# Reading score tables back tile by tile behind the scatters, and attention of the last tile in pieces, in a two-layer graph network on one Trainium2 core

## The reference, cut to what matters

```python
# edges come sorted by dst; dst is drawn as 625 * u**2, so low nodes have the most edges
xl = (x @ W_l).reshape(625, 4, 64)
xr = (x @ W_r).reshape(625, 4, 64)
e = xl[src] + xr[dst]
e = where(e >= 0, e, 0.2 * e)
score = einsum('ehd,hd->eh', e, att)              # 20000 edges x 4 heads
m = segment_max(score, dst)
ex = exp(score - m[dst])
alpha = ex / (segment_sum(ex, dst)[dst] + 1e-16)
agg = segment_sum(alpha[:, :, None] * xl[src], dst)
h = elu(agg + bias) + x
gnn = layernorm(h) * gamma + beta
...
x = x + gnn + mix(xn)
logits = layernorm(x) @ gate_w + gate_b           # top 2 of 16 experts
...
```

## Time and profile before

| | |
|---|---|
| median of three runs | 1079.36 us (1077.4 to 1082.58) |
| profiled execution, its own time | 1083.8 us |
| span of its trace | 1082.0 us |
| mean granted TensorE clock | 0.877 |
| busy: PE, DVE, ACT, POOL | 851.8, 774.3, 353.6, 380.2 us |
| 16 DMA engines, mean over the span | 120 GB/s |

### The profile page before, as it was taken

One profiled execution on the slowest core, in us unless ns is written; L12 is line 12 of the kernel. 1 busy time (PEld: TensorE's weight loads), 2 busy tenths in 40 slices (PEclk: granted clock), 3 DMA queues, 4 the chain that ended last, 5 costly groups with the idle time before them and its releaser, 6 DMA issues.

```text
span 1082.0 us, 18242 instructions
## 1 busy us (share of the span) xinstructions
PE 851.8 (79%) x5483; PEld 744.8 (69%) x5483; DVE 774.3 (72%) x1980; ACT 353.6 (33%) x1004; POOL 380.2 (35%) x321
## 2 busy tenths in 40 slices
PE   4888778977999880078459999769893895799996
PEld 2578666766778770078359999755793685788985
DVE  7778878788775880079888887576979656766635
ACT  0377444444663452056011111001560171121120
POOL 3288476776777677200022222410000000311204
PEclk9988889887999995577669999888897897799999
DMA  8830000000000000593059999750000001788883
GB/s 290 260 129 2 2 3 3 3 4 2 4 3 3 3 3 2 137 237 91 24 182 331 322 331 330 253 193 1 1 2 0 1 2 32 293 291 300 303 312 98
DMA packets 38278, 129.35 MB, mean 120 GB/s; under 512 B 12885, under 2 KB 20929, under 8 KB 29913
## 3 DMA queue, kind: packets, MB, share of 16 engines
q1 hardware_dynamic: 21742, 112.64, 31.3%
q0 software_dynamic: 10464, 8.67, 4.8%
q10 hardware_dynamic: 5992, 7.04, 1.9%
HBM read 108.83 MB, written 19.26 MB: 118 GB/s over the span
## 4 chain that ended last, share of the span: by engine, by line
PE 54%; DVE 23%; DMA 10%; issue 6%; POOL 4%; ACT 2%; SPq 0%; DVEq 0%; POOLq 0%; ACTq 0%
PE bank L862 12%; PE bank L651 7%; PE bank L873 6%; PE bank L583 4%; PE bank L795 3%; DMA arena<-pair_scores 3%; POOL arena L2281 2%; DVE tc L1281 2%; PE bank L629 2%; DMA pair_scores<-arena,pair_cells 2%; PE bank L961 2%; PE bank L784 2%; DVE cnt L1275 2%; PE bank L669 2%; DVE arena L1287 2%
## 5 line engine op out<-in xcount | busy, mean ns | idle before, releaser
L2247 POOL DMA_INDIRECT pair_scores<-arena,pair_cells x184 | 230.0, 1250 | 107.5 <-issue 57.3
L2271 POOL DMA_INDIRECT arena<-row_tab,ids x42 | 57.6, 1371 | 498.6 <-DVE ids L1664 491.7
L862 PE MATMUL bank<-arena 128*128 128x128 f32 x1480 | 182.5, 282 | 2.8 <-DMA arena<-in_exp 2.8
L862 PEld LDWEIGHTS bank<-arena 128*128 128x128 f32 x1480 | 177.1, 199 | 4.2 <-DMA arena<-in_exp 3.1
L651 PE MATMUL bank<-x_hi,hot 125*125 x368 | 119.6, 350 | 6.5 <-issue 0.7
L2011 ACT ACTIVATE tc<-bank 125x256 f32<-125x256 f32 x184 | 70.7, 385 | 136.4 <-PE bank L651 126.1
L651 PE MATMUL bank<-x_lo,hot 125*125 x368 | 106.1, 307 | 0.0
L873 PE MATMUL bank<-arena 128*128 128x256 f32 (+1 forms) x404 | 97.4, 384 | 0.0
L784 PE MATMUL bank<-ident,arena 125*125 125x125 f32 x260 | 46.0, 310 | 65.1 <-ACT arena L2058 63.7
L651 PEld LDWEIGHTS bank<-x_hi,hot 125*125 125x125 f32 x368 | 76.9, 209 | 20.1 <-issue 17.7
L784 PEld LDWEIGHTS bank<-ident,arena 125*125 125x125 f32 x260 | 41.2, 219 | 69.6 <-issue 57.7
(11 more groups left out here) (395 smaller groups left out, 1693.0 us busy)
## 6 DMA issues: line engine op xcount, KB each, us to landing
arena<-in_exp SPq DMA_DIRECT2D x25, 1024.0 KB, 6.8
arena<-in_exp SPq DMA_DIRECT2D x17, 1386.0 KB, 6.3
arena<-in_exp0o SPq DMA_DIRECT2D x25, 512.0 KB, 6.9
pair_scores<-cnt SPq DMA_DIRECT2D x10, 1093.8 KB
arena<-in_exp1o SPq DMA_DIRECT2D x17, 640.0 KB
arena<-pair_scores SPq DMA_DIRECT2D x7, 1093.8 KB
slot_y<-arena ACTq DMA_DIRECT2D x34, 128.0 KB, 6.3
fmaps<-pair_scores SPq DMA_DIRECT2D x3, 1093.8 KB
```

Of the source, the lines that this page charges most:

```text
L862: mm = pe.matmul(banks[1 + 2 * q + buf][0:rows, i * SLOTS:(i + 1) * SLOTS], w_in(s, q, k, m, rows), xsT[:, s, k, :], start=(k == 0), stop= ...
L2247: p.indirect_dma_start(out=pair_scores[which], in_=sc_ring[:, i, which, :], in_offset=None, out_offset=bass.IndirectOffsetOnAxis(ap=pair_c ...
L2271: p.indirect_dma_start(out=xs[:, q, :], out_offset=None, in_=tab, in_offset=bass.IndirectOffsetOnAxis(ap=ids[:, q, :], axis=0))\
```

## The change

SP no longer waits for all scatters. It reads from `ends_i` how many scatters of each table have to land until the blocks of a tile are complete; with these edges 38, 53, 66 and 76 of 92 for tiles 0 to 3, and 78, 80, 82 and 84 for the first four src pieces of tile 4. `ends_i` is a new row of eight integers, made in the sort by one more matmul on PE and five small operations on DVE. Tile m is loaded when its count is reached and its buffers are free (`h2` counts up to 3 at the three steps of the mix block named above, whose memory the new buffers share). The load of a tile is cut into pieces of 32, 32, 32 and 29 rows for each table (`PACED`), and each DMA is issued when the one before has landed, one at a time. The last tile comes in five pieces by src tile, of 112 and 13 rows x 2,000 B for each table, the fifth after all scatters; its maxima are taken over four pieces first and over the fifth behind them (`last_maxima`). The ring `masked` gets a fourth slot in this layer. The order on DVE, and the cut of the transposes ahead of the gate (`LATE`: tiles 0 to 3, then tile 4, in place of `CHUNKS`: tiles 0 to 2, then 3 and 4), follow from that.

```diff
+BASES["ends"] = BASES["order"] + BUCKETS
+ENDS = [T * m for m in range(1, T)] + [T * (T - 1) + s for s in range(1, T)]
+PACED = tuple(slice(r, min(r + 32, P)) for r in range(0, P, 32))
+LATE = [(0, (T - 1) * P, tuple(range(T - 1))), ((T - 1) * P, P, (T - 1,))]
...
-        SDENSE = [(0, 1), (5, 6), (2, 3), (4, 1), (0, 6)]
+        SDENSE = [("a0", "tde"), ("f1", "f0"), ("a1", "a2"), ("a3", "tab"), ("f0", "a2")]
...
+                at = BASES["ends"]
+                pe.matmul(banks[4][0:1, 2 * SORTED:2 * SORTED + len(ENDS)], begins, orders[:, at:at + len(ENDS)],
+                          start=True, stop=True).then_inc(sem("sorted"), 1)
...
+                rounded_of(ends_f[:, :], banks[4][0:1, 2 * SORTED:2 * SORTED + len(ENDS)], 0.5, -0.25)
+                own.link(v.tensor_scalar(ends_f[:, :], ends_f[:, :], 16.0, 16.0, ALU.mult, ALU.add))
+                v.tensor_scalar(ends_i[:, :], ends_f[:, :], float(16 * PAIRS), None, ALU.min).then_inc(sem("sorting"), 1)
...
+                    if i == MIX["m2"]:
+                        dve.sem_inc(sem("h2"), 1)
...
+            def merge_piece(s):
+
+                dve.wait_ge(sem(f"sdense{T - 1}"), (s + 1 if s == T - 1 else T - 1) * 2 * 16 * len(PARTS))
+                first, second = (sdense[q][:, s * P:(s + 1) * P, :] for q in SDENSE[T - 1])
+                own.note(v.tensor_tensor(first, first, second, ALU.max))
+
+            def last_maxima(part):
...
+                for h in range(H):
+                    i = m * H + h
+                    a, b, low = (0, cut, rneg) if part == 0 else (cut, N, rneg_a)
+                    after(dve, sem("l0_prob"), i - 3)
+                    own.note(v.tensor_tensor_reduce(masked_l0[:, i % 4, a:b], first[:, a:b, h], cnt[:, m, a:b], -1.0, -LOWEST,
+                                                    ALU.add, ALU.min, low[:, i:i + 1]))
+                    if part == 1:
+                        own.fence()
+                        v.tensor_tensor(rneg[:, i:i + 1], rneg[:, i:i + 1], rneg_a[:, i:i + 1], ALU.min)\
+                            .then_inc(sem("l0_max"), 1)
...
             average(2)
             add_elu(1)
-            table_maxima(4)
+            for s in range(T - 1):
+                merge_piece(s)
             average(3)
             add_elu(2)
-            add_normed(0, 1, 2)
-            average(4)
+            last_maxima(0)
             add_elu(3)
-            add_elu(4)
-            add_normed(3, 4)
-            norm_again(*range(T))
+            merge_piece(T - 1)
+            last_maxima(1)
+            add_normed(0, 1, 2, 3)
+            average(T - 1)
+            norm_again(0, 1, 2, 3)
+            add_elu(T - 1)
+            add_normed(T - 1)
+            norm_again(T - 1)
+            late_from_fm(0)
...
+            def await_scatters(end):
+
+                landed = sp.value_load(ends_i[0:1, end:end + 1], min_val=8, max_val=16 * PAIRS)
+                for w in range(2):
+                    sp.wait_ge(sem(f"scattered{w}"), landed)
+
+            def load_table(m):
+
+                n = 0
+                for w in range(2):
+                    for rows in PACED:
+                        sp.dma_start(sdense[SDENSE[m][w]][rows, :, :].rearrange("p n h -> p (n h)"), cells[w][m][rows])\
+                            .then_inc(sem(f"sdense{m}"), 16)
+                        n += 16
+                        sp.wait_ge(sem(f"sdense{m}"), n)
...
+            sp.wait_ge(sem("sorting"), SORTING["ends"])
+            sp.wait_ge(sem("h2"), 1)
+            await_scatters(0)
+            load_table(0)
+            sp.wait_ge(sem("h2"), 2)
+            await_scatters(1)
+            load_table(1)
+            sp.wait_ge(sem("h2"), 3)
+            await_scatters(2)
+            load_table(2)
+            await_scatters(3)
+            load_table(3)
+            sp.wait_ge(sem("merged"), 3)
+            for s in range(T - 1):
+                await_scatters(T - 1 + s)
+                load_piece(s)
+            sp.wait_ge(sem(f"sdense{T - 1}"), (T - 1) * 2 * 16 * len(PARTS))
             for w in range(2):
                 sp.wait_ge(sem(f"scattered{w}"), 16 * PAIRS)
...
+            load_piece(T - 1)
```

More of the change, by code:

```diff
@@ L920, in ranks @@
                 mm.then_inc(done, 1)
-            for c, (off, w, tiles) in enumerate(CHUNKS):
+            for c, (off, w, tiles) in enumerate(LATE):
                 pe.wait_ge(sem("xn"), T + tiles[-1] + 1)
@@ L1519, in norm_again, with late_from_fm @@
                         .then_inc(sem("xn"), 1)
+            def late_from_fm(c):
+                off, w, _ = LATE[c]
+                bank, freed = got(dve, ("xnT1", 1, c))
+                v.tensor_copy(fa[:, 1, off:off + w], bank[:, 0:w]).then_inc(freed, 1)
             table_maxima(0)
@@ L1529, in _, with route @@
             add_elu(1)
[L1530 removed]
+            for s in range(T - 1):
+                merge_piece(s)
             average(3)
             add_elu(2)
[L1533 to L1534 removed]
+            last_maxima(0)
             add_elu(3)
[L1536 to L1538 removed]
+            merge_piece(T - 1)
[7 more added lines that the diff above has]
+            late_from_fm(0)
             read_out(dve, "l0", "agg")
             dve.wait_ge(sem("xn"), 2 * T)
[L1542 removed]
+            def route(name, gate_name, ne, nblk, bias, eps, ahead=None):
                 for t in range(T):
+                    if ahead is not None and t == T - 2:
+                        ahead()
                     bank, freed = got(dve, (gate_name, t))
@@ L1733, in experts @@
                         then(t)
-            from_fm("xnT1", fa)
-            shift_logits, shares = route("e0", "gate0", NE0, NBLK0, vec[0:P, V_GATEB:V_GATEB + NE0], 0.0)
+            shift_logits, shares = route("e0", "gate0", NE0, NBLK0, vec[0:P, V_GATEB:V_GATEB + NE0], 0.0,
+                                         lambda: late_from_fm(1))
             experts("e0", NBLK0, UNITS0, shift_logits, shares, lambda t: own.note(v.bn_stats(stats[:, t, :], x[:, t, :])))
@@ L2051, in attend @@
             def attend(name, tiles_of):
+                prob, probT = probs[name]
+                lifted = lambda i: masked_l0[:, i % 4, :] if name == "l0" else masked[:, i % 3, :]
                 def exponentials(i):
@@ L2057, in exponentials @@
                         read_out(act, name, "pT", i - 3)
-                    a.activation(prob[:, i % 3, 0:w], masked[:, i % 3, 0:w], ACT.Exp, bias=rneg[:, i:i + 1],
+                    a.activation(prob[:, i % 3, 0:w], lifted(i)[:, 0:w], ACT.Exp, bias=rneg[:, i:i + 1],
                                  scale=-1.0, accum_out=rden[:, i:i + 1]).then_inc(sem(name + "_prob"), 1)
@@ L2156, in _ @@
             attend("l0", all_tiles)
-            from_fm("xnT1", fa)
+            for c, (off, w, _) in enumerate(LATE):
+                bank, freed = got(act, ("xnT1", 0, c))
+                a.activation(fa[:, 0, off:off + w], bank[:, 0:w], ACT.Copy).then_inc(freed, 1)
             shares("gate0", NE0)
@@ new lines, in load_piece @@
+            def load_piece(s):
+                m = T - 1
+                for w in range(2):
+                    for rows in PARTS:
+                        sp.dma_start(sdense[SDENSE[m][w]][rows, s * P:(s + 1) * P, :].rearrange("p n h -> p (n h)"),
+                                     cells[w][m][rows, s * P * H:(s + 1) * P * H]).then_inc(sem(f"sdense{m}"), 16)
+            sp.wait_ge(sem("sorting"), SORTING["ends"])
+            sp.wait_ge(sem("h2"), 1)
+            await_scatters(0)
+            load_table(0)
@@ L2330, in _ @@
                 sp.wait_ge(sem(f"scattered{w}"), 16 * PAIRS)
[L2332 to L2341, removed]
@@ L2466 @@
         "base": columns_before,
-        "order": np.concatenate([one_of, cell_steps, tile_steps, earlier], axis=1),
+        "order": np.concatenate([one_of, cell_steps, tile_steps, earlier, np.eye(BUCKETS, dtype=np.float32)[:, ENDS]],
+                                axis=1),
         "vec0": np.concatenate([v.reshape(-1) for v in l0]),
```

51 lines of the change are left out of this document (32 added, 19 removed).

## The result

The changed kernel takes 1100.9 us (median of four runs, 1092.49 to 1103.19) beside 1080.97 us of the kernel before; the ratio is 1.0166, with a 95% interval of 1.0095 to 1.0237. It is slower by 1.7%. Forecast were 1069 us and a range of 1042 to 1092: wrong in sign, and outside the range. The profiled execution took 1099.26 us with a span of 1097.5.

The account below looks back on a forecast made before the run. DVE's 48.39 us wait for tables loaded behind the last scatter was taken as the bound; gate 11.3 us earlier less 0.6 for the sort gives 10.7, from 1079.4 to 1069 us (62 in 100), range 1042 to 1092.

Parts of the forecast that it names:

- the 29 rows: Early table loads: a 29-row load runs on one engine and takes 13.2 us, against 3.2 us for 32 rows.
- the first rival: Early loads: all 16 engines share the 29 rows, 3.2 us a load, 1034 us in all; 12 in 100.
- the slower engine: 29-row loads: one engine slower than its share, 0.67 us a row, 21.9 us a load, 1120 us; 4 in 100.
- DVE's wait for table 3: After the pairs end, DVE uses tables 0 to 2, then idles about 33 us until table 3 lands near 472.
- Hidden, by 12 us: Scatters beside loads: the last lands near 479, hidden because landings up to 491.8 us cost nothing.
- its count: Scatters beside loads: 61 issued from 334.9 us on, 59 of them in the 136.7 us of the loads.
- the pitch: Scatter issues beside early loads: 2.3 us apart, with landings of about 4.3 us.
- the table: Paced early loads: 22.8 us a half table, 45.6 a table, so table 3 lands at 471.7 us.
- The tail: From the fifth piece's maxima at 496.0 to the gate's end at 528.8: 32.8 us; gate 11.3 earlier than before.
- The 0.6 us for the sort's operations: Sort: five more DVE operations and a matmul cost 0 to 1.2 us, taken as 0.6.
- The held scatters: Scatters queue behind big rows, landing in 7 us; last lands near 516, gate 553, time 1093; 20 in 100.
- the last sign of being wrong: DVE's timeline: a hole ahead of the fifth piece's merge that ends with the last scatter would refute the forecast.

Follow-up runs that it names:

- e6: Changed kernel with its 29-row loads, waiting for 86 scatters of each table instead of all 92; 1090.87 us, 1.0064 of the kernel before.
- e3: Changed kernel with all table loads behind the last scatter, in 112 and 13 rows, unpaced; 1091.46 us, 1.0056 of the kernel before.
- e1: Changed kernel with the 29-row slice cut into 16 and 13 rows; 1057.79 us, 0.9718 of the kernel before.
- e5: e1 with the fifth piece waiting for 86 scatters of each table, leaving out 12 spare columns; 1042.72 us, 0.9592 of the kernel before.
- e7: e1 with DVE waiting for all scatters ahead of its first table; 1095.96 us in its one run.

## Why the prediction was wrong

**Right: the 29 rows.** They take 13.9 us (13.2 forecast) and close on one engine. The reading of the small packets in the earlier trace rows held, and these packets agree with the Trainium skill's rule ("DMA: Bandwidth & Descriptors", "Why a DMA increments its semaphore by 16 and not by 1") beside which it was set. With 13.9 us the first rival (3.2) and the slower engine (21.9) fall. DVE's wait for table 3 is where the forecast put it, 40.9 us long instead of 33; the 8.6 ahead of table 2 stood in no forecast.

**The step that failed: "Hidden, by 12 us".** The last scatter was put near 479 and hidden up to 491.8; it lands at 519.3. Two terms of it were too small, and a third was missing. First, its count: 61 scatters were taken as left at 334.9, as in the kernel before. Table 0 had by then delayed them: column 104 is issued at 321.27 instead of 303.72, and at 335.52 the trace shows 72 left, not 61 (POOL's timeline, the first line from the kernel before):

```profile
303.72 1.50 POOL L2247 DMA_INDIRECT pair_scores<-arena,pair_cells  x1 [0.77 <-issue]
...
321.27 1.19 POOL L2315 DMA_INDIRECT pair_scores<-arena,pair_cells  x1 [0.78 <-DVE arena L1309]
...
335.52 1.19 POOL L2315 DMA_INDIRECT pair_scores<-arena,pair_cells  x1 [0.70 <-issue]
```

I had treated POOL as waiting for pairs there, but its waits for DVE in that stretch are too short to take 17 us back. Second, the pitch (the time from one scatter's issue to the next): columns 112 to 171 are issued from 335.52 to 488.38, 2.59 us apart, not 2.3. Landings of the loads' four stretches have medians of 5.0, 3.9, 4.7 and 4.8 us, where 4.3 was taken. They part by the kind of load: the landings of scatters issued while 29 rows come in (448.2 to 462 us), then while loads of 32 rows do (462.1 to 473.2), with DVE idle in both, are:

```profile
DMA to landing us min/median/max: 3.5/5.8/6.1
```

```profile
DMA to landing us min/median/max: 3.1/3.5/4.2
```

The 5.8 are 3.2 more than the 2.6 of the earlier trace rows: by estimate some eight rows of 0.39 us each (13.9 less the forecast's 2.5 fixed, over 29). The Trainium skill's rule that an engine changes queues only after several descriptors ("DMA: Bandwidth & Descriptors", "Queues, rings and completion order") agrees with that; how many were taken at a time no run here shows.

Third, POOL itself was held beside DVE: all 184 scatters take 243.9 us of POOL instead of 230.2. No term stood for that; the last section has the rows.

**A mis-sized term: the table.** 45.6 us was forecast for a table; from 336.5 to 488.3 three tables take 151.8, 50.6 each. The loads of 32 rows take 3.4 to 3.7 instead of 3.2, those of 29 rows 13.9 and 15.1 in table 3. That is 15 us for three tables, with 1.6 of a later start: 16.6 us on the landing of table 3 (488.3, forecast 471.7). In e6, which has no hole ahead of the fifth piece, the gate is 16.3 us behind the 528.8 of the forecast: that is this term, for table 3 is merged there 15.5 us behind it. The margin of the forecast, 11.3 us, was less than its own error on three tables that follow one another.

**The tail** was 32.8 us from the fifth piece's maxima to the gate; 31.8 were measured (524.56 to 556.35). From the last of the four pieces to the fifth merge 10.9 were forecast, 10.2 measured. The 0.6 us for the sort's operations no run shows: in e3, which has them, the first merge starts at 457.72 beside 457.66.

**The rivals.** The held scatters, at 20 in 100, came true in place and nearly in price (last landing 516 forecast, 519.3 measured; gate 553 and 556; time 1093 and 1100.9), and with them the last sign of being wrong that the forecast named: a hole ahead of the fifth piece's merge that ends with the last scatter. That the figures lie so near is partly luck, since the rival's reason was right in part only: landings of 7 us were not needed, since the delay had begun with table 0, the loads lasted longer, and DVE held POOL. What I should have done is to run the count of scatters from the first early load on, and not from the second.

## What to carry to other kernels

Before a load is cut into slices, look at how many engines each slice will run on: 32, 32, 32, 29 rows cost 4 to 5% against 32, 32, 32, 16, 13 (the ratios of the changed kernel and e1, of e6 and e5), through its own time and through what queues behind it. Early reading beside a chain of small transfers that wait for each other is a trade: count the delay of the chain from the first read on, and ask what the end of the chain is still waited for. Here its last 14 links wrote cells that no one reads, and leaving 12 of them out of the wait was worth 21 us where the tables come late and 15 where they come early.

## What was not expected of the hardware

A scatter that POOL issues while DVE merges or takes maxima of a table is held: on POOL 1.19 us becomes 1.9 to 3.7. The one of 488.38 us ends at 492.11, 1.06 us after the merge of 488.29 to 491.05 is over. e7, which keeps the tables' work on DVE away from the scatters, shows none above 1.66 us from 400 us on. The Trainium skill ("SBUF — State Buffer", "SBUF: two separate sides") states that a DVE operation with two inputs in SBUF and a POOL operation that reads SBUF exclude each other for a whole instruction; these rows agree with it, if a scatter counts as an operation that reads SBUF, as its operands in the rows, `arena` and `pair_cells`, suggest. Which access is held no run here shows.
